# Stacking key halves for the query-key products and moving row statistics to ScalarE in a gated cross-attention and expert kernel

## The chip, the cores and the metric

One core of a Trainium2 chip runs the whole program in one launch. The metric is the device time of that launch in microseconds (us), lower is better. TensorE does the matrix products, VectorE, ScalarE and GpSimd the elementwise work, SyncE only issues DMAs. The profile names them PE, DVE, ACT, POOL and SP.

## The reference

Input: 32 batches of 256 rows with 256 features, and for each batch 77 context rows with 192 features. The layer is a gated cross-attention with 8 heads of 64, then a gated mixture of experts:

```python
q = (layernorm(x) @ Wq).reshape(b, n, 8, 64)
k = (context @ Wk).reshape(b, m, 8, 64)
v = (context @ Wv).reshape(b, m, 8, 64)
attn = softmax(einsum('bihd,bjhd->bhij', q, k) * 64 ** -0.5)
x = x + tanh(g_xattn) * (einsum('bhij,bjhd->bihd', attn, v).reshape(...) @ Wout + bout)
y = layernorm(x)
x = x + tanh(g_ffn) * (top-2 of 16 gated experts of y + shared gated expert of y)
```

All arrays are float32. The last line, the expert part, is not touched by the change.

## The kernel before

**Products in halves.** A float32 product is made from rounded halves. Each operand is split into a rounded part `hi` (an ACT copy into a rounded 32-bit format, helper `high`, L226) and the remainder `lo` (a DVE subtraction, helper `low`, L231). The helper `products` (L71) then issues three matmuls into one PSUM bank: hi x hi (L75), one half's lo (L76) and the other half's lo (L77).

**The algebra.** The scores of one head are x Wq_h K_h^T. The kernel never makes the queries: it makes K = context Wk for a pair of heads (128 rows, 64 for each head), and from it M_h = Wq_h K_h^T for each head, for four batches at once (4 x 77 = 308 columns). The scores are then x times M. The layer norm of x enters as follows: the mean is taken out of Wq once, and the reciprocal standard deviation of each row, `rstd1`, is the scale of the exponential.

**How Wq is laid out.** `wq_hi` and `wq_lo` hold 128 partitions for each head; 64 of them are that head's rows and the other 64 are zeros, because `kT` holds two heads on its 128 partitions. A *query-key unit* (`query_keys`, L281) is the product of half of one head's Wq (128 columns) with `kT`: three matmuls of 128x308.

**Stages.** `prepare` (L332) loads and splits the weights, makes K and M for the first group of four batches and the statistics of the first 16 tiles of 128 rows. `attend` (L550) runs 8 groups g of 4 batches; b is the batch and q its place in the group. `mix` and `passes` are the expert part.

**One batch of `attend`.** The order on each engine is written out by hand, and semaphores tie the engines together. TensorE, for batch b: scores of the first 128 rows; two query-key units for the next group; attention times values of batch b-1 (`attend_values`, 24 matmuls in two banks); scores of the second 128 rows; two more query-key units; transposes of the first half's probabilities (8, L723); the output projection of b-1 (24 matmuls); K for a pair of heads (5 matmuls); V of this batch (5 matmuls); transposes of the second half's probabilities. Units are made in groups 0 to 6 and K in 27 of the 32 batches (groups 0 to 5, and three batches of group 6).

ScalarE, in this order: `xT_hi`, `ctxb_hi`, two `M_hi`, the exponential of the first half (L782), two `OT_hi`, two `M_hi`, the exponential of the second half, two `PT_hi` of the first half, `kT_hi`, `V_hi`, two `PT_hi` of the second half.

VectorE, in this order: `row_max` (L834) and the subtraction of it (L837) for the first half, two `M_lo`, one `bn_stats`, `row_sum` (L844) and its reciprocal (L847), two `OT_lo`; then the same with `row_max`, the subtraction, two `M_lo`, one `bn_stats` and `row_sum` for the second half, two `PT_lo` of the first half, the residual of b-1 (two additions and two `bn_stats`), `kT_lo`, `V_lo`, two `PT_lo` of the second half. PT is the transposed probabilities, OT the attention output, transposed.

GpSimd makes xT_lo and other remainders, multiplies the probabilities by 1 / row_sum (L646), adds the bias, and at the end of a group turns the statistics into `rstd1` with 20 small chained instructions (`rstd_on_gpsimd`, L138).

**Statistics ahead.** In groups 0 to 5 SyncE loads, for batch b, the 256 rows of batch b+8 into `x_ahead` (two buffers). `stats_ahead` (L873) makes their mean and variance with two `bn_stats` on VectorE, one for each 128 rows.

**Waits that matter here.** `attend_values` of b waits for the last `PT_lo` of b and for `V_lo`. A query-key unit waits for `kT_lo` (K_lo) and for its bank to be read (M_lo). Transposes wait for GpSimd's normalisation and for the `PT_lo` that reads the same bank. `row_max` waits for the scores.

Of the kernel before, what the change touches and what calls it, by code (L numbers as in the profile page):

```python
# [28 lines left out]
P = 128  # L29
# [9 lines left out]
GB = 4  # L39
# [95 lines left out]
LN_STEPS = 6 + 2 + 3 * 4  # L135


def rstd_on_gpsimd(nc, pool, stats, rstd, var, work, chain, before):  # L138
# [8 lines left out]
    g = nc.gpsimd  # L147
    link(g.tensor_tensor(work, stats[:, :, 1], stats[:, :, 4], ALU.subtract))
    link(g.tensor_tensor(work, work, work, ALU.mult))
    link(g.tensor_scalar(work, work, 0.25, LN_EPS, ALU.mult, ALU.add))  # L150
    link(g.tensor_tensor(var, stats[:, :, 2], stats[:, :, 5], ALU.add))
    link(g.tensor_scalar(var, var, 1.0 / D, None, ALU.mult))
    link(g.tensor_tensor(var, var, work, ALU.add))
# [8 lines left out]

def attention_tensors(nc, c, ctx):
# [5 lines left out]
    a.kT = [sb(f"kT_{s}", [P, GK], F32R) for s in ("hi", "lo")]  # L169
# [6 lines left out]
    a.stats1 = sb("stats1", [P, TILES * 6])  # L176
# [117 lines left out]
def make_M(nc, pe, c, a, n, pair, k):  # L294
    pe.wait_ge(a.K_lo, n + 1)
    wait(pe, a.M_lo, 4 * n + k - 1)
    query_keys(nc, c, a, a.ps_proj[k % 2][:, 0:GK], a.kT, pair, k)


def high_K(nc, act, a, n):  # L300
    act.wait_ge(a.K_done, n + 1)
    wait(act, a.M_done, 4 * n)
    high(nc, a.kT[0][:, :], a.ps_proj[1][:, 0:GK], a.K_hi)


# [26 lines left out]
def prepare(nc, c, a):  # L332
# [5 lines left out]
    with ExitStack() as ctx:  # L338
# [3 lines left out]
        kT = [a.kT, [sb(f"kT2_{s}", [P, GK], F32R) for s in ("hi", "lo")]]  # L342
# [20 lines left out]
        def head_rows(w, j):  # L363

            return w[j * DH:(j + 1) * DH, :].rearrange("p (q j) d -> p q j d", j=2)[:, :, j, :]

        with nc.Block() as block:  # L367
# [34 lines left out]
            def _(pool):  # L402
# [3 lines left out]
                for w in (c.wq_hi, c.wq_lo):  # L406
                    nc.gpsimd.memset(f32(w[:, :, :]), 0.0).then_inc(zeroed, 1)
# [25 lines left out]
            def _(pe):  # L433
# [14 lines left out]
                key_unit(1)  # L448
                pe.wait_ge(wq_lo_done, 2)
# [10 lines left out]
            def _(act):  # L460
# [37 lines left out]
            def _(v):  # L498
# [51 lines left out]
def attend(nc, c, a):  # L550


    with ExitStack() as ctx:
# [7 lines left out]
        var1, work1 = sb("var1", [P, 4 * GB]), sb("work1", [P, 4 * GB])  # L561
        ps_proj = a.ps_proj
# [17 lines left out]
        ahead_stats, rstd_chain, rstd_ready = sem("ahead_stats"), sem("rstd_chain"), sem("rstd_ready")  # L580
# [17 lines left out]
        with nc.Block() as block:  # L598
# [42 lines left out]
            def _(pool):  # L641
# [7 lines left out]
                def rstd_of(first, tiles, before):  # L649
                    stats = a.stats1[:, bass.ds(first * 6, tiles * 6)].rearrange("p (t s) -> p t s", s=6)  # L650
# [1053 lines left out]
```

## Time and profile before

| what | value |
|---|---|
| time, median of 3 runs (lowest to highest) | 1077.92 us (1070.39 to 1084.31) |
| time of the profiled execution | 1068.79 us |
| its span, first to last instruction | 1066.6 us |
| mean granted clock of TensorE | 0.95 of full speed |
| busy: TensorE, VectorE, ScalarE, GpSimd | 86%, 75%, 44%, 47% |

The span of the profiled execution is 2.2 us shorter than its own time; what is outside is start and end of the launch. `prepare` runs from 0 to about 34 us, `attend` to about 503 us, the expert part to the end. In timeline rows the first number is the start in us from the span's start, the second the length in us; a merged row (x2, x4) gives the whole length of its instructions. What stands in square brackets is the idle time of that engine before the row and what ended it. The end of a matmul is modelled, so the pace of TensorE is read from the starts of successive rows, not from their lengths.

### The profile page before, as it was taken

Reading aid. Unit: us, or ns where it says so; the run is one execution under the profiler, and the core shown is the slowest. Engines: PE = TensorE matmul, PEld = TensorE weight load, DVE = VectorE, ACT = ScalarE, POOL = GpSimd, SP = SyncE. Lnnn points to the kernel's source line nnn. Section 1 sums busy time; section 2 is a strip of 40 time slices with the busy share of each in tenths; the row PEclk is TensorE's granted clock in tenths of the full one; section 3 lists DMA queues with packets and bytes.
Section 4 is the critical chain, followed back from the end, with each engine's and each line's share of the span. In section 5 each row is a group of like instructions: output and inputs, shape, how many; then the busy total and the mean of one; then the engine's idle time right before and its main releaser. Section 6 shows DMA issues by size and latency. Waiting matters only on the chain. (4 is left out here: it accounts for less than half of the span.)

```text
span 1066.6 us, 20998 instructions
## 1 busy us (share of the span) xinstructions
PE 916.2 (86%) x6728; PEld 857.1 (80%) x6729; DVE 797.5 (75%) x1824; ACT 471.9 (44%) x967; POOL 506.0 (47%) x635
## 2 busy tenths in 40 slices
PE   4799999999999999997599999973868784788883
PEld 3699999999999999986588888862857773778783
DVE  5699999999899999886588888882636563466563
ACT  4456555555555555542644554430323231333331
POOL 7546453545545454441235555551435545155555
PEclk9799999999999999999599999996989998799997
DMA  7213232222323211211524444455887872767660
GB/s 221 68 44 97 86 98 86 72 74 81 98 86 97 74 54 57 66 53 60 173 94 172 162 168 166 149 209 199 317 298 254 279 252 82 238 213 220 216 202 23
DMA packets 108326, 150.94 MB, mean 142 GB/s; under 512 B 21830, under 2 KB 72394, under 8 KB 108240
## 3 DMA queue, kind: packets, MB, share of 16 engines
q1 hardware_dynamic: 92880, 107.60, 33.0%
q0 software_dynamic: 15360, 42.24, 10.4%
q8 instruction: 49, 0.80, 0.3%
q14 instruction: 37, 0.30, 0.1%
HBM read 90.19 MB, written 65.90 MB: 146 GB/s over the span
## 5 line engine op out<-in xcount | busy, mean ns | idle before, releaser
L646 POOL TENSOR_TENSOR prob<-prob,row_sum 128x616 f32<-128x616 f32 x64 | 77.9, 1217 | 132.9 <-DVE row_sum L847 132.6
L1482 POOL DMA_INDIRECT rows_scratch<-prow x80 | 78.7, 984 | 98.0 <-DVE prow L1618 78.9
L75 PE MATMUL ps_h<-w_flat,eyT_hi 128*128 x320 | 98.8, 309 | 27.6 <-DVE eyT_lo L1600 24.3
L1482 POOL DMA_INDIRECT out<-prow x80 | 78.7, 983 | 76.9 <-DVE prow L1618 53.5
L1575 ACT ACTIVATE eyT_hi<-ps_ey 128x512 fp32r<-128x512 f32 x80 | 48.2, 602 | 145.9 <-PE ps_ey L1504 90.9
L1074 POOL DMA_INDIRECT rows_scratch<-row,slot x64 | 67.9, 1061 | 75.5 <-DVE row L1321 60.9
L1504 PE MATMUL ps_ey<-ident,prow 128*128 128x128 f32 x320 | 52.2, 289 | 51.2 <-DMA prow<-rows_scratch 44.2
L1600 DVE TENSOR_TENSOR eyT_lo<-ps_ey,eyT_hi 128x512 fp32r<-128x512 f32 x80 | 54.9, 686 | 54.3 <-ACT eyT_hi L1575 52.2
L1618 DVE TENSOR_TENSOR prow<-ps_z,prow 128x512 f32<-128x512 f32 x80 | 54.7, 685 | 53.4 <-PE ps_z L77 26.5
L76 PE MATMUL ps_h<-w_flat,eyT_hi 128*128 x320 | 91.1, 285 | 0.0
L77 PE MATMUL ps_h<-w_flat,eyT_lo 128*128 x320 | 90.8, 284 | 0.0
L75 PEld LDWEIGHTS ps_h<-w_flat,eyT_hi 128*128 128x128 f32 x320 | 62.6, 196 | 33.4 <-issue 33.0
L75 PE MATMUL ps_s<-M_hi,xT_hi 128*128 128x308 f32 x256 | 81.1, 317 | 5.0 <-PEq L367 4.1
L262 POOL TENSOR_TENSOR xT_lo<-xT_raw,xT_hi 128x512 fp32r<-128x512 f32 x32 | 41.3, 1289 | 92.5 <-ACT ctxb_hi L228 91.4
L1504 PEld LDWEIGHTS ps_ey<-ident,prow 128*128 128x128 f32 x320 | 38.3, 148 | 55.3 <-DMA prow<-rows_scratch 45.6
L1607 DVE SCALAR_TENSOR_TENSOR a<-ps_h,prow,silu 128x128 f32<-128x128 f32 x160 | 48.4, 344 | 43.9 <-issue 18.5
L233 DVE TENSOR_TENSOR PT_lo<-ps_pt,PT_hi 77x512 fp32r<-77x512 f32 x128 | 80.3, 667 | 0.0
L76 PE MATMUL ps_s<-M_lo,xT_hi 128*128 128x308 f32 x256 | 78.4, 306 | 0.0
L77 PE MATMUL ps_s<-M_hi,xT_lo 128*128 128x308 f32 x256 | 78.3, 306 | 0.0
L75 PE MATMUL ps_o<-wo_hi,OT_hi 128*128 128x256 f32 x256 | 74.6, 291 | 1.4 <-DVE OT_lo L233 1.4
L75 PE MATMUL ps_o<-PT_hi,V_hi 96*128 96x256 f32 x256 | 72.9, 285 | 3.3 <-DVE PT_lo L233 3.3
L228 ACT ACTIVATE M_hi<-ps_proj 128x308 fp32r<-128x308 f32 x112 | 47.7, 429 | 56.7 <-PE ps_proj L77 56.1
(263 smaller groups left out, 3418.0 us busy)
## 6 DMA issues: line engine op xcount, KB each, us to landing
prow<-rows_scratch SPq DMA_DIRECT2D x160, 258.0 KB
rows_scratch<-blank SPq DMA_DIRECT2D x34, 258.0 KB, 2.9
xT_raw<-in_xT SPq DMA_DIRECT2D x32, 256.0 KB, 4.4
x_tok<-in_x SPq DMA_DIRECT2D x32, 256.0 KB, 2.9
x_scratch<-x_tok SPq DMA_DIRECT2D x32, 256.0 KB, 3.2
row<-x_scratch SPq DMA_DIRECT2D x16, 512.0 KB, 3.9
x_ahead<-in_x SPq DMA_DIRECT2D x26, 256.0 KB, 4.4
w_raw<-in_W SPq DMA_DIRECT2D x16, 256.0 KB
```

The source lines that it names most:

```text
L75: nc.tensor.matmul(out, lh, rh, start=start and n == 0, stop=False)
L76: nc.tensor.matmul(out, lh, rl, start=False, stop=False)
L77: last = nc.tensor.matmul(out, ll, rh, start=False, stop=stop and n == len(pairs) - 1)
L233: nc.vector.tensor_tensor(lo, source, f32(hi), ALU.subtract).then_inc(done, 1)
L646: nc.gpsimd.tensor_tensor(pr, pr, row_sum[i][:, :].unsqueeze(2).broadcast_to((P, H, CK)), ALU.mult).then_inc(normed, 1)
L1074: pool.indirect_dma_start(c.rows1, bass.IndirectOffsetOnAxis(slot1[:, t:t + 1], 0), row[G % NX][:, i, :], None).then_inc(scattered[G % NX] ...
L1482: pool.indirect_dma_start(dram, bass.IndirectOffsetOnAxis(target, 0), row[u][:, i, 0:columns], None, bounds_check=bound, oob_is_err=False) ...
L1504: last = nc.tensor.transpose(ps_y[u % 2][:, k, i * P:(i + 1) * P], row[u][:, i, YROW + k * P:YROW + (k + 1) * P], c.ident[:, :])
L1575: nc.scalar.activation(yT[p][0][:, :, :], ps_y[p][:, :, :], ACT.Copy).then_inc(yT_hi, 1)
L1600: V.tensor_tensor(yT[p][1][:, :, :], ps_y[p][:, :, :], f32(yT[p][0][:, :, :]), ALU.subtract).then_inc(yT_lo, 1)
L1607: V.scalar_tensor_tensor(a[p][:, i, :], ps_h[p][:, i, 0:HID], row[b][:, i, weight:weight + 1], silu[p][:, i, :], ALU.mult, ALU.mult).then_ ...
L1618: V.tensor_tensor(row[b][:, :, 0:D], ps_z[p][:, :, :], row[b][:, :, 0:D], ALU.add).then_inc(final, 1)
```

## The change

Two parts.

**Keys and remainder in one operand.** `kT` is now one tile for each of the two heads of a pair. For head 0 its partitions 0 to 63 hold the rounded keys and partitions 64 to 127 hold the remainder of the same keys; for head 1 it is the other way round. `wq_hi` holds a head's rows in both halves of the partitions, `wq_lo` in the one half that meets the rounded keys, with zeros in the other. A query-key unit is two matmuls: Wq_hi times the stacked operand gives hi x hi + hi x lo, Wq_lo times it gives lo x hi. To write it, each K needs two ACT copies and two DVE subtractions of 64x308 where one of each of 128x308 stood. In `prepare`, ScalarE writes `wq_hi` with four copies of 64x1024 (two before), and GpSimd clears only `wq_lo`.

**Statistics on ScalarE.** The two `bn_stats` of a batch of groups 0 to 5 leave VectorE. ScalarE issues four activations of 128x256 with an accumulator output in their place: Identity with scale -1/256 for two tiles (minus the mean), and Square with the minus mean as bias for two tiles (the sum of squares). Their elementwise outputs go to unused bfloat16 tiles. They stand between the exponential of the second half and the `PT_hi` of the first half. GpSimd's chain for these groups has 15 instructions in place of 20. The statistics in `prepare` stay on VectorE.

```diff
 def query_keys(nc, c, a, out, kT, pair, k):
-    h, cc = 2 * pair + k // 2, k % 2
-    products(nc, out, [
-        (c.wq_hi[:, h, cc * P:(cc + 1) * P], c.wq_lo[:, h, cc * P:(cc + 1) * P],
-         kT[0][:, :], kT[1][:, :])]).then_inc(a.M_done, 1)
+    h, cc, both = 2 * pair + k // 2, k % 2, kT[k // 2][:, :]
+    nc.tensor.matmul(out, c.wq_hi[:, h, cc * P:(cc + 1) * P], both, start=True, stop=False)
+    nc.tensor.matmul(out, c.wq_lo[:, h, cc * P:(cc + 1) * P], both, start=False, stop=True).then_inc(a.M_done, 1)
+
+def half(j):
+    return slice(j * DH, (j + 1) * DH)
+
+def high_keys(nc, a, kT, bank):
+    for j in range(2):
+        high(nc, kT[j][half(j), :], bank[half(j), :], a.K_hi)
+
+def low_keys(nc, v, a, n, kT, bank):
+    for j in range(2):
+        v.wait_ge(a.K_hi, 2 * n + j + 1)
+        low(nc, kT[j][half(1 - j), :], kT[j][half(j), :], bank[half(j), :], a.K_lo)
...
 def make_M(nc, pe, c, a, n, pair, k):
-    pe.wait_ge(a.K_lo, n + 1)
+    pe.wait_ge(a.K_lo, 2 * n + 2)
...
+                def stats_ahead(b, b_half, par):
+                    act.wait_ge(a.ahead_in[par], 16 * (b_half + 1))
+                    for i in range(2):
+                        t = 2 * (b + 2 * GB) + i
+                        nc.scalar.activation(unused[i][:, :], a.x_ahead[par][:, i, :], ACT.Identity, scale=-1.0 / D,
+                                             accum_out=less_mean[:, t:t + 1]).then_inc(ahead_mean, 1)
+                    wait(act, ahead_stats, 2 * b)
+                    for i in range(2):
+                        t = 2 * (b + 2 * GB) + i
+                        act.wait_ge(ahead_mean, 2 * b + i + 1)
+                        nc.scalar.activation(unused[2 + i][:, :], a.x_ahead[par][:, i, :], ACT.Square,
+                                             bias=less_mean[:, t:t + 1],
+                                             accum_out=squares[:, t:t + 1]).then_inc(ahead_stats, 1)
...
                         exponentials(b, 1)
+                        if exists(g + 2):
+                            stats_ahead(b, 2 * g + q // 2, q % 2)
                         high_PT(b, 0)
...
                             low_M_units(b, g, q, 0)
-                        if exists(g + 2):
-                            stats_ahead(b, 2 * g + q // 2, q % 2, 0)
                         sums(b, 0)
...
                             low_M_units(b, g, q, 1)
-                        if exists(g + 2):
-                            stats_ahead(b, 2 * g + q // 2, q % 2, 1)
                         sums(b, 1)
```

The next rows are ScalarE's instructions of `attend` from the exponential of a batch's second half on, in the kernel before; L228 is the helper `high`.

```order
L782 ACTIVATE prob<-prob,rstd 128x616
L228 ACTIVATE PT_hi<-ps_pt 77x4x128 x2
L228 ACTIVATE kT_hi<-ps_proj 128x308
L228 ACTIVATE V_hi<-ps_proj 77x4x2x64
L228 ACTIVATE PT_hi<-ps_pt 77x4x128 x2
```

The same place in the changed kernel, where L246 is `high` and L816 the exponential:

```order
L816 ACTIVATE prob<-prob,rstd 128x616
L829 ACTIVATE unused,less_mean<-x_ahead 128x256
L829 ACTIVATE unused,less_mean<-x_ahead 128x256
L835 ACTIVATE unused,squares<-x_ahead,less_mean 128x256
L835 ACTIVATE unused,squares<-x_ahead,less_mean 128x256
L246 ACTIVATE PT_hi<-ps_pt 77x4x128 x2
L246 ACTIVATE kT<-ps_proj 64x308
L246 ACTIVATE kT<-ps_proj 64x308
L246 ACTIVATE V_hi<-ps_proj 77x4x2x64
L246 ACTIVATE PT_hi<-ps_pt 77x4x128 x2
```

Four activations now stand ahead of `PT_hi`, and the copy of the keys is two.

VectorE's instructions from the subtraction of the second half's maximum to the next batch's `row_max`, in the kernel before:

```order
L837 TENSOR_TENSOR prob<-ps_s,row_max 128x616
L233 TENSOR_TENSOR M_lo<-ps_proj,M_hi 128x4x77 x2
L876 BN_STATS stats<-x_ahead 128x6
L844 TENSOR_REDUCE row_sum<-prob 128x8
L847 RECIPROCAL row_sum<-row_sum 128x8
L233 TENSOR_TENSOR PT_lo<-ps_pt,PT_hi 77x4x128 x2
L858 TENSOR_TENSOR x_tok<-ps_o,x_tok 128x256
L861 BN_STATS stats<-x_tok 128x6
L858 TENSOR_TENSOR x_tok<-ps_o,x_tok 128x256
L861 BN_STATS stats<-x_tok 128x6
L233 TENSOR_TENSOR kT_lo<-ps_proj,kT_hi 128x308
L233 TENSOR_TENSOR V_lo<-ps_proj,V_hi 77x4x2x64
```

And in the changed kernel, where L251 is `low`:

```order
L888 TENSOR_TENSOR prob<-ps_s,row_max 128x616
L251 TENSOR_TENSOR M_lo<-ps_proj,M_hi 128x4x77 x2
L895 TENSOR_REDUCE row_sum<-prob 128x8
L898 RECIPROCAL row_sum<-row_sum 128x8
L251 TENSOR_TENSOR PT_lo<-ps_pt,PT_hi 77x4x128 x2
L909 TENSOR_TENSOR x_tok<-ps_o,x_tok 128x256
L912 BN_STATS stats<-x_tok 128x6
L909 TENSOR_TENSOR x_tok<-ps_o,x_tok 128x256
L912 BN_STATS stats<-x_tok 128x6
L251 TENSOR_TENSOR kT<-ps_proj,kT 64x308 x2
L251 TENSOR_TENSOR V_lo<-ps_proj,V_hi 77x4x2x64
```

The `bn_stats` behind `M_lo` is gone (so is the one in the first half of the batch), and the subtraction of the keys is two.

## Rows read from the trace of the kernel before

**Rows 1.** The page: TensorE's granted clock in 40 slices of the span.

```profile
PEclk9799999999999999999599999996989998799997
```

**Rows 2.** Busy time by stretch: groups 0 to 5, 6, and 7.

```profile
core 0: us, PE busy (x) PEld busy (x) DVE busy (x) ACT busy (x) POOL busy (x), PEclk, DMA share, GB/s
...
64.00:180.00 116.00, 116.00 (x885) 112.42 (x884) 107.48 (x210) 66.15 (x131) 56.87 (x93) 1.00 0.29 84
...
411.00:440.00 29.00, 29.00 (x221) 27.98 (x221) 25.95 (x50) 16.20 (x32) 11.37 (x13) 1.00 0.21 61
...
453.90:493.00 39.10, 37.91 (x283) 34.69 (x282) 32.26 (x58) 17.62 (x33) 14.86 (x15) 1.00 0.16 50
```

**Rows 3.** Timeline of DVE in group 2, from one second half to the next.

```profile
203.48 0.80 DVE L834 TENSOR_REDUCE row_max<-ps_s 128x8 f32<-128x616 f32 x1 [0.36 <-PE ps_s L77]
...
205.03 0.85 DVE L233 TENSOR_TENSOR M_lo<-ps_proj,M_hi 128x308 fp32r<-128x308 f32 x2
205.80 0.42 DVE L876 BATCH_NORM_STATS2 stats<-x_ahead 128x6 f32<-128x256 f32 x1
...
207.06 1.24 DVE L233 TENSOR_TENSOR PT_lo<-ps_pt,PT_hi 77x512 fp32r<-77x512 f32 x2
...
217.94 0.80 DVE L834 TENSOR_REDUCE row_max<-ps_s 128x8 f32<-128x616 f32 x1 [0.38 <-PE ps_s L77]
```

**Rows 4.** Timeline of PE in group 2, one query-key unit.

```profile
203.28 0.31 PE L75 MATMUL ps_proj<-kT_hi,wq_hi 128*128 128x308 f32 x1
203.42 0.31 PE L76 MATMUL ps_proj<-kT_lo,wq_hi 128*128 128x308 f32 x1
```

**Rows 5.** Timeline of DVE in group 7, with neither units, keys nor statistics ahead.

```profile
461.31 0.80 DVE L834 TENSOR_REDUCE row_max<-ps_s 128x8 f32<-128x616 f32 x1 [0.30 <-PE ps_s L77]
...
464.77 1.23 DVE L233 TENSOR_TENSOR PT_lo<-ps_pt,PT_hi 77x512 fp32r<-77x512 f32 x2
...
469.29 0.79 DVE L834 TENSOR_REDUCE row_max<-ps_s 128x8 f32<-128x616 f32 x1
...
474.30 0.80 DVE L834 TENSOR_REDUCE row_max<-ps_s 128x8 f32<-128x616 f32 x1 [0.33 <-PE ps_s L77]
```

**Rows 6.** Timeline of PE in group 7, the first matmul of `attend_values`.

```profile
469.42 0.39 PE L75 MATMUL ps_o<-PT_hi,V_hi 96*128 96x256 f32 x1 [0.41 <-DVE PT_lo L233]
```

**Rows 7.** Timeline of ACT in group 2.

```profile
205.14 0.81 ACT L782 ACTIVATE prob<-prob,rstd 128x616 f32<-128x616 f32 x1 [0.39 <-DVE prob L837]
205.86 1.06 ACT L228 ACTIVATE PT_hi<-ps_pt 77x512 fp32r<-77x512 f32 x2
...
211.36 0.63 ACT L228 ACTIVATE xT_hi<-xT_raw 128x512 fp32r<-128x512 f32 x1
211.89 0.33 ACT L228 ACTIVATE ctxb_hi<-ctxb_raw 128x154 fp32r<-128x154 f32 x1
```

**Rows 8.** Groups by form, 60 to 480 us: busy us, mean ns of one, idle before.

```profile
L228 ACT ACTIVATE PT_hi<-ps_pt 77x512 fp32r<-77x512 f32 x119 | 63.3, 582 | 0.0
...
L228 ACT ACTIVATE ctxM_hi<-ctx_raw 128x616 fp32r<-128x616 f32 x6 | 4.3, 714 | 0.0
```

**Rows 9.** Timeline of `prepare`: the shortest activation, with two columns.

```profile
13.22 0.20 ACT L469 ACTIVATE tanh_g<-gates 128x2 f32<-128x2 f32 x1 [2.99 <-DMA bias<-in_bout]
```

**Rows 10.** Timeline of DVE: second halves of batches 0, 1, 26 and 27.

```profile
43.97 0.75 DVE L834 TENSOR_REDUCE row_max<-ps_s 128x8 f32<-128x616 f32 x1
...
59.13 0.80 DVE L834 TENSOR_REDUCE row_max<-ps_s 128x8 f32<-128x616 f32 x1 [0.36 <-PE ps_s L77]
...
420.75 0.80 DVE L834 TENSOR_REDUCE row_max<-ps_s 128x8 f32<-128x616 f32 x1 [0.37 <-PE ps_s L77]
...
435.19 0.80 DVE L834 TENSOR_REDUCE row_max<-ps_s 128x8 f32<-128x616 f32 x1 [0.38 <-PE ps_s L77]
```

**Rows 11.** Timeline of DVE at the end of `prepare`.

```profile
32.92 0.41 DVE L516 BATCH_NORM_STATS2 stats<-x_ahead 128x6 f32<-128x256 f32 x1
```

**Rows 12.** Timeline of PE: the first scores of `attend`.

```profile
34.63 0.59 PE L75 MATMUL ps_s<-M_hi,xT_hi 128*128 128x308 f32 x1 [4.11 <-PEq L367]
```

More of the change, by code:

```diff
@@ L135, with linked @@
 LN_STEPS = 6 + 2 + 3 * 4
-def rstd_on_gpsimd(nc, pool, stats, rstd, var, work, chain, before):
+LN_AHEAD_STEPS = 1 + 2 + 3 * 4
+def linked(pool, chain, before):
     step = [0]
@@ L145, in link, with newton @@
         pool.wait_ge(chain, before + step[0])
[L147 to L153, printed above, removed]
+    return link
+def newton(g, link, rstd, var, work):
     link(g.tensor_scalar(rstd.bitcast(I32), var.bitcast(I32), -0.5, float(SEED), ALU.mult, ALU.add))
@@ L160, in rstd_on_gpsimd, with rstd_of_stats, rstd_of_squares @@
         link(g.tensor_tensor(rstd, rstd, work, ALU.mult))
+def rstd_of_stats(nc, pool, stats, rstd, var, work, chain, before):
+    g, link = nc.gpsimd, linked(pool, chain, before)
+    link(g.tensor_tensor(work, stats[:, :, 1], stats[:, :, 4], ALU.subtract))
+    link(g.tensor_tensor(work, work, work, ALU.mult))
+    link(g.tensor_scalar(work, work, 0.25, LN_EPS, ALU.mult, ALU.add))
+    link(g.tensor_tensor(var, stats[:, :, 2], stats[:, :, 5], ALU.add))
+    link(g.tensor_scalar(var, var, 1.0 / D, None, ALU.mult))
+    link(g.tensor_tensor(var, var, work, ALU.add))
+    newton(g, link, rstd, var, work)
+def rstd_of_squares(nc, pool, squares, rstd, var, work, chain, before):
+    g, link = nc.gpsimd, linked(pool, chain, before)
+    link(g.tensor_scalar(var, squares, 1.0 / D, LN_EPS, ALU.mult, ALU.add))
+    newton(g, link, rstd, var, work)
 def attention_tensors(nc, c, ctx):
@@ L402, in _ @@
             def _(pool):
-                for w in (c.wq_hi, c.wq_lo):
-                    nc.gpsimd.memset(f32(w[:, :, :]), 0.0).then_inc(zeroed, 1)
+                nc.gpsimd.memset(f32(c.wq_lo[:, :, :]), 0.0).then_inc(zeroed, 1)
                 pool.wait_ge(wk_hi_done, 1)
@@ L463, in _ @@
                 high_group(nc, act, a, 0)
-                act.wait_ge(zeroed, 2)
                 act.wait_ge(centred, 4)
-                for j in range(2):
-                    high(nc, head_rows(c.wq_hi, j), wq_raw[j * DH:(j + 1) * DH, :, :], wq_hi_done)
+                for at in (0, 1):
+                    for j in range(2):
+                        high(nc, head_rows(c.wq_hi, j, j ^ at), wq_raw[half(j), :, :], wq_hi_done)
                 act.wait_ge(gates_in, 48)
@@ L561, in attend @@
         var1, work1 = sb("var1", [P, 4 * GB]), sb("work1", [P, 4 * GB])
+        less_mean, squares = sb("less_mean", [P, TILES]), sb("squares", [P, TILES])
+        unused = [sb(f"unused{i}", [P, D], BF16) for i in range(4)]
         ps_proj = a.ps_proj
```

48 lines of the change are left out of this document (22 added, 26 removed).

## The prediction

> **What bounds the kernel now.** I read the busy time by stretch first, since the change touches only `prepare` and `attend`. In groups 0 to 5 TensorE is busy for 116.00 of 116.00 us, VectorE for 107.48, ScalarE for 66.15 [rows 2]. So TensorE bounds `attend`, with VectorE close behind. The timeline of VectorE then gives the period of a batch: the second half's `row_max` starts at 203.48 and again at 217.94, 14.46 us apart, and both times VectorE had waited 0.36 to 0.38 us for TensorE's scores [rows 3]. A full engine says nothing of the chain behind it, so the next thing to find is the loop through the other engines and how far it is below 14.46.
>
> Group 7 shows that loop bare. It has no units, no keys and no statistics, and there TensorE waits 0.41 us for `PT_lo` in each batch [rows 6]. One turn, from `row_max` at 461.31: (1) subtraction, exponential, `row_sum`, reciprocal, until `PT_lo` starts at 464.77: 3.46. (2) VectorE alone, with `PT_lo`, residual, `V_lo`, `PT_lo` in one run until the next `row_max` at 469.29: 4.52. (3) to the first matmul of `attend_values` at 469.42: 0.13 [rows 6]. (4) TensorE makes `attend_values` and scores, and the next second-half `row_max` starts at 474.30: 4.88. Together 12.99, exactly 474.30 less 461.31 [rows 5].
>
> In group 2 the same loop has one `kT_lo` more in part (2). A pair of `M_lo` of the same shape moves VectorE on by 0.77 (205.03 to 205.80), so one costs 0.39. Part (1) is 207.06 less 203.48 = 3.58 [rows 3]. That gives 3.58 + 4.91 + 0.13 + 4.88 = 13.50. So 0.96 us of slack lie under TensorE's 14.46.
>
> **TensorE's side.** One matmul of a unit starts 0.14 us behind the other (203.28, 203.42) [rows 4]; its length of 0.31 overlaps with the next. Each batch loses four of them, 0.57 us, so TensorE's own period falls to 13.89. Over the 28 batches with units that is at most 16 us, 1.5% of the time.
>
> **VectorE's side.** Two `bn_stats` leave; one moves the engine on by about 0.33, but `row_sum` behind it must still wait for the exponential (0.81 from 205.14 to 205.95 [rows 7]), so the second one gives only about 0.1 in part (1). The second subtraction of keys adds 0.39: it has half the partitions, but as many columns, 308, and I take the time by columns. The first `bn_stats` and its DMA wait are off this loop.
>
> **ScalarE's side, which decides.** The four activations stand between the exponential and `PT_hi`, and the engine works in order. Before, the exponential starts 1.66 us after `row_max` (203.48, 205.14), `PT_hi` follows 0.72 later at 205.86 [rows 3, 7], and the first one takes 0.58 [rows 8] plus 0.04 to wake VectorE, which is assumed: no row here prices the step alone, and the 0.13 of part (3) is above it. With S for the four activations `PT_lo` can start 1.66 + 0.72 + S + 0.58 + 0.04 = 3.00 + S after `row_max`. `row_sum` has long been done by then, so this takes the place of part (1). The changed loop is
>
> 3.00 + S + (4.52 + 0.77) + 0.13 + 4.88 = 13.30 + S.
>
> It equals the old period at S = 1.16 and TensorE's new one at 0.59.
>
> What is S? An activation of 154 columns takes 0.33 and one of 512 takes 0.63, so 256 take 0.42; the next starts 0.10 before the end (211.89 against 211.99) [rows 7], which leaves 0.32. The Square takes its bias from a tile. The exponential takes its scale from one and needs 0.81 for 616 columns [rows 7], where a copy of 616 needs 0.714 [rows 8]: 0.10 more, 0.41. So the four are 0.64 + 0.82 = 1.46 without the accumulator. No row of this trace shows what writing an accumulator costs. The nearest is the shortest activation, two columns in 0.20 [rows 9]: overlapped as the others it moves the engine on by 0.10, with nothing overlapped on either side 0.30. It can also be free. I take 0.10, since the other activations overlap: S = 1.86, with ends at 1.28 (no pointer cost either, four times 0.32) and 2.66. The waits on `ahead_mean` cost nothing I can see: the mean of tile 0 is made while that of tile 1 runs. The load of `x_ahead` has the whole batch to land.
>
> So the period becomes 15.16, +0.70. VectorE then waits about 1.2 us for `PT_hi` in each batch, and TensorE stands still for 15.16 - 13.89 = 1.27 us ahead of `attend_values` and the unit that waits for `V_lo`.
>
> **The sum.** Statistics run in batches 0 to 23. The step from batch 0 to 1 takes 15.16 already (43.97 to 59.13) [rows 10] and has no residual, so it hides them: 23 steps of +0.70 = +16.1. In group 6 there are none, and the period of 14.44 (420.75 to 435.19) [rows 10] is TensorE's; the loop there is 12.99 + 0.77 = 13.76, below 13.87. Three steps win 0.57: -1.7. Group 7 has no units: 0. In `prepare` five K cost VectorE 0.39 more each, up to 1.9; VectorE ends at 33.33 [rows 11], `attend` begins at 34.63 [rows 12], and the matmuls saved there are behind it, so I take +1.1 with ends 0 and 1.9. The extra `wq_hi` copies are ahead of keys that come later, the shorter GpSimd chain is off the loop: 0. The sum is +15.5 us.
>
> The profiled execution took 1068.79, so its like would be 1084.3. It is 9.1 below the median of the runs, 1077.92; the same +15.5 on the median gives 1093.4, which I predict. That is 1.4% up. A measurement of this kernel tells about 2% from no change, 21.6 us.
>
> Bounds: S = 1.28 gives +0.12 a batch, +2.8 - 1.7 + 0 = +1, 1079. S = 2.66 gives +1.50 a batch, +34.5 - 1.7 + 1.9 = +34.7, 1112.6. Runs scatter by some us, so I give 1076 to 1111.
>
> **Rivals.**
>
> *The accumulator costs more (chance 0.25).* If each output costs 0.17 or more, S passes 2.12 and the kernel is slower by over 2%. At 0.25 each, S = 2.46: +1.30 a batch, 29.9 - 1.7 + 1.1 = +29, 1107. For it: the write depends on the very activation before it, so overlap is not sure. Against: in these rows neighbours overlap also where one is tiny work.
>
> *The statistics are short, and the kernel is not slower (0.18).* Place: the same four activations; price: S; it decides at S = 1.16. Output to bfloat16, or an accumulating pass that writes faster, could halve the 0.83 ns a column: 0.21 and 0.31 each, 1.04 with a free accumulator. Then the loop is 14.34: 23 times -0.12 = -2.8, -1.7, +1.1 = -3.4, 1074.5. For it: no row has a bfloat16 output. Against: the columns per ns are the same here for copies and the exponential, within 0.10 in 616. Even S = 0 would win only 23 x 0.57 + 1.7 - 1.1 = 14 us, 1.3%, so faster by over 2% needs something I don't see.
>
> *The clock (0.05).* The granted clock stays at 1.00, the level of 2.4 GHz, through group 7, though TensorE is idle there for 1.2 of 39.1 us in waits of 0.4 [rows 2]; it is below the top in slices around the start of `attend` [rows 1], where TensorE stands still for 4.11 us at once [rows 12]. The changed kernel has 1.27 us of them in each batch. At 1.2 GHz part (4) would be longer by up to 4.7, so a tenth of the stretch at that level costs 0.5 a batch, +11: 1104. The Trainium skill (TensorE: Matmul & The Clock Gate, "A second HAM failure mode: psum-queue depth-cycling") speaks against the change here: frequent short idles between groups of matmuls can make the clock swing between its levels. By that rule the time would be the 1104; the trace, at 1.00 with idles of 0.4 us, does not bear it out so far.
>
> **How the numbers follow.** Forecast 0.52, rivals 0.25, 0.18 and 0.05. Slower by over 2%: the first rival and half of the third, 0.28. Faster by over 2%: 0.02. Within 2%: 0.70.
>
> **What would show it.** Right: timeline rows of VectorE with an idle of 1.0 to 1.5 us before `PT_lo` of the first half, ended by ScalarE's `PT_hi`; four activations moving ScalarE on by 1.86 in all; TensorE waiting for `PT_lo` ahead of `attend_values`; `row_max` 15.1 to 15.2 us apart in groups 0 to 5, 13.9 in group 6, 13.0 in group 7; TensorE's share below 93% there. Wrong: no idle before `PT_lo`, or a period at or below 14.4 in groups 1 to 5 (then S or the loop is wrong); 64x308 subtractions that take half the time; a clock below 1.00 inside `attend`; a change of time in the expert part, of which I expect none.

## The result and the profile after

| | time before | time after | ratio, 95% interval |
|---|---|---|---|
| median | 1077.93 us (4 runs, 1070.39 to 1084.31) | 1101.96 us (4 runs, 1097.02 to 1105.34) | 1.0224 (1.0190 to 1.0258) |

The kernel became slower by 24.0 us. That it is slower is clear of the scatter; whether by more than 2% is not, since the interval holds 1.02. The forecast was 15.5 us; 1101.96 lies inside the range given. The profiled execution took 1097.02 us, its span is 1095.3 us.

The busy time of groups 0 to 5 and of 42 us of group 6, in the changed kernel, answers to [rows 2]:

```profile
core 0: us, PE busy (x) PEld busy (x) DVE busy (x) ACT busy (x) POOL busy (x), PEclk, DMA share, GB/s
64.00:180.00 116.00, 107.48 (x791) 100.31 (x789) 101.33 (x191) 75.57 (x188) 50.84 (x79) 1.00 0.29 84
411.00:453.00 42.00, 42.00 (x317) 40.09 (x317) 39.50 (x76) 24.90 (x51) 16.47 (x17) 1.00 0.21 62
```

TensorE, full before, is busy for 107.48 of 116.00 us (92.7%). It is idle for 8.5 us there, and its granted clock is still 1.00. No engine is full in this stretch any more. So the bound is no engine but a chain through several, and the share of busy time can't name it. The timeline of VectorE in group 2 does; it answers to [rows 3]:

```profile
213.33 0.80 DVE L885 TENSOR_REDUCE row_max<-ps_s 128x8 f32<-128x616 f32 x1 [0.31 <-PE ps_s L77]
...
214.88 0.85 DVE L251 TENSOR_TENSOR M_lo<-ps_proj,M_hi 128x308 fp32r<-128x308 f32 x2
215.84 0.80 DVE L895 TENSOR_REDUCE row_sum<-prob 128x8 f32<-128x616 f32 x1
216.67 0.20 DVE L898 RECIPROCAL row_sum<-row_sum 128x8 f32<-128x8 f32 x1
218.11 1.29 DVE L251 TENSOR_TENSOR PT_lo<-ps_pt,PT_hi 77x512 fp32r<-77x512 f32 x2 [1.23 <-ACT PT_hi L246]
...
220.54 0.43 DVE L912 BATCH_NORM_STATS2 stats<-x_tok 128x6 f32<-128x256 f32 x1
221.00 0.98 DVE L251 TENSOR_TENSOR kT<-ps_proj,kT 64x308 fp32r<-64x308 f32 x2
222.01 0.69 DVE L251 TENSOR_TENSOR V_lo<-ps_proj,V_hi 77x512 fp32r<-77x512 f32 x1
...
223.81 0.78 DVE L885 TENSOR_REDUCE row_max<-ps_s 128x8 f32<-128x616 f32 x1
...
228.82 0.80 DVE L885 TENSOR_REDUCE row_max<-ps_s 128x8 f32<-128x616 f32 x1 [0.32 <-PE ps_s L77]
```

Read it as the loop of the prediction. Part (1), 213.33 to 218.11, is 4.78. It ends with an idle of 1.23 us for ScalarE's `PT_hi`, which [rows 3] do not have. Part (2), to `row_max` at 223.81, is 5.70; the rest, to 228.82, is 5.01. The period is 15.49, where it was 14.46.

The same place on ScalarE, which answers to [rows 7]:

```profile
215.00 0.81 ACT L816 ACTIVATE prob<-prob,rstd 128x616 f32<-128x616 f32 x1 [0.64 <-DVE prob L888]
215.72 0.40 ACT L829 ACTIVATE unused<-x_ahead 128x256 bf16<-128x256 f32 x1
216.02 0.19 ACT L829 ACTIVATION_READ_ACCUMULATOR unused<-x_ahead 128x1 f32 x1
216.12 0.40 ACT L829 ACTIVATE unused<-x_ahead 128x256 bf16<-128x256 f32 x1
...
216.51 0.49 ACT L835 ACTIVATE unused<-x_ahead,less_mean 128x256 bf16<-128x256 f32 x1
216.91 0.19 ACT L835 ACTIVATION_READ_ACCUMULATOR unused<-x_ahead,less_mean 128x1 f32 x1
217.01 0.49 ACT L835 ACTIVATE unused<-x_ahead,less_mean 128x256 bf16<-128x256 f32 x1
...
217.50 1.06 ACT L246 ACTIVATE PT_hi<-ps_pt 77x512 fp32r<-77x512 f32 x2
```

`PT_hi` starts at 217.50, where the first of the four activations starts at 215.72: they cost 1.78 us, forecast 1.86. Each accumulator output is an instruction of its own in the trace, 0.19 long, and moves the engine on by 0.09 to 0.10.

The waits of all `attend` (60 to 500 us), by what ended them:

```profile
engine line waited for: us in total, times, longest us
...
DVE PT_lo L251 <- ACT PT_hi L246: 28.3, 23, 1.2
...
PE ps_proj L302 <- DVE V_lo L251: 16.2, 23, 0.7
...
PE ps_o L75 <- DVE PT_lo L251: 9.2, 25, 0.4
DVE row_max L885 <- PE ps_s L77: 9.0, 29, 0.3
```

Reading it from top to bottom gives the loop: ScalarE is late for VectorE, VectorE for TensorE, TensorE for VectorE's next `row_max`. The first row has 23 waits, one for each batch with statistics from 1 to 23.

**Where the 24 us came from.** The second half's `row_max` of a batch dates it in both traces. In the changed kernel it starts at 44.66 (batch 0), 58.54 (1), 414.65 (24), 457.00 (27) and 508.87 (31); in the kernel before at 43.97, 59.13, 391.91, 435.19 and 487.28 (rows of the same timeline; [rows 10] have three of them).

| stretch | forecast | measured |
|---|---|---|
| `prepare` and batch 0, to its second `row_max` | +1.1 | +0.7 |
| step 0 to 1 | 0 | -1.3 (13.88 for 15.16) |
| steps 1 to 24, 23 of them | +16.1 | +23.3 |
| steps 24 to 27 | -1.7 | -0.9 (42.35 for 43.28) |
| steps 27 to 31 | 0 | -0.2 |
| expert part, from batch 31 | 0 | +7.1, in this one execution |

The last row is within the scatter: experiments 1 to 4 below, with the same expert part, took 595, 581, 584 and 579 us for it; before took 579 and after 586. By the difference of the medians, 24.0, about 2 us are left for it. What the sum missed lies in the third row, and it is 0.31 us in each batch.

### The profile page after: what moved, and what is told of

The parts are those of the page before. It is cut to its first block and busy times, and to the rows that moved or that the text cites. A ratio compares the mean times of both kernels' runs of the same rounds, so it can differ in the third digit from the quotient of the medians.

```text
span 1095.3 us, 20944 instructions
## 1 busy us (share of the span) xinstructions
PE 917.8 (84%) x6600; PEld 847.1 (77%) x6601; DVE 802.6 (73%) x1808; ACT 522.7 (48%) x1193; POOL 497.1 (45%) x604
## 5 line engine op out<-in xcount | busy, mean ns | idle before, releaser
L75 PE MATMUL ps_h<-w_flat,eyT_hi 128*128 x320 | 101.0, 316 | 31.2 <-DVE eyT_lo L1641 25.3
L251 DVE TENSOR_TENSOR PT_lo<-ps_pt,PT_hi 77x512 fp32r<-77x512 f32 x128 | 81.5, 676 | 29.6 <-ACT PT_hi L246 29.6
L76 PE MATMUL ps_h<-w_flat,eyT_hi 128*128 x320 | 93.6, 293 | 0.0
L77 PE MATMUL ps_h<-w_flat,eyT_lo 128*128 x320 | 93.1, 291 | 0.0
L816 ACT ACTIVATE prob<-prob,rstd 128x616 f32<-128x616 f32 x64 | 51.9, 811 | 74.6 <-DVE prob L888 74.6
L75 PE MATMUL ps_o<-PT_hi,V_hi 96*128 96x256 f32 x256 | 76.3, 298 | 11.8 <-DVE PT_lo L251 11.7
L246 ACT ACTIVATE M_hi<-ps_proj 128x308 fp32r<-128x308 f32 x112 | 41.9, 426 | 71.2 <-PE ps_proj L303 71.2
```

The lines of the kernel that those rows point to most:

```text
L75: nc.tensor.matmul(out, lh, rh, start=start and n == 0, stop=False)
L76: nc.tensor.matmul(out, lh, rl, start=False, stop=False)
L77: last = nc.tensor.matmul(out, ll, rh, start=False, stop=stop and n == len(pairs) - 1)
L251: nc.vector.tensor_tensor(lo, source, f32(hi), ALU.subtract).then_inc(done, 1)
L816: nc.scalar.activation(prob[i][:, :], prob[i][:, :], ACT.Exp, scale=c.rstd1[:, bass.ds(2 * b + i, 1)]).then_inc(exp_done, 1)
```

## The experiments

All ratios are against the kernel before, on the same chip. The first four kernels ran on a chip where the kernel before takes 1075.39 us, close to the runs above; experiments 5 and 7 ran on a second (1016.80 us) and 6 and 8 on a third (1019.86 us). The periods in `attend` agree between the chips (in group 7, which no edit touches, a batch takes 12.94 to 13.01 us in every experiment after its first step), so experiments are compared by their periods and by ratios, never by times across chips. What no edit touches reads the same on both: the idle before `PT_lo` is 1.23 in experiment 5 as in the change, and parts (3) and (4) are 4.98 for 5.01. Three theories stood at the start. The place: the four activations cost the time because they are ahead of `PT_hi` in ScalarE's order. The work: ScalarE or a slower product would cost it anywhere. For what was missed in part (2): a price of the key subtractions.

**1. The four activations elsewhere** (`e1_stats_behind_OT`). The same instructions, ahead of the second half's `M_hi`, where ScalarE waited for TensorE (69.0 us of such waits in `attend`).

```diff
                             high_OT(b - 1)
+                        if exists(g + 2):
+                            stats_ahead(b, 2 * g + q // 2, q % 2)
                         if not last:
                             high_M_units(b, g, q, 1)
                         exponentials(b, 1)
-                        if exists(g + 2):
-                            stats_ahead(b, 2 * g + q // 2, q % 2)
                         high_PT(b, 0)
```

> The four statistics activations move from ahead of the first half's PT_hi to behind OT_hi, where ScalarE waits about 1.4 us for TensorE's units in the changed kernel. Theory (the loop through PT_hi: its place on ScalarE is what costs): PT_lo of the first half starts 3.46 us after row_max again, the loop is 3.46 + 5.70 + 5.01 = 14.1 to 14.2 us in groups 0 to 5, the same as in group 6, against 15.49; the time falls by 1.33 x 23 = 31 us under the changed kernel, to about 0.7 to 0.9% under the kernel before. Rival (the amount of work given to ScalarE costs, wherever it stands, or the waits of TensorE for V_lo come from elsewhere): the period stays at 15 us or above and the kernel stays slower than before.

Measured: 1067.17 us, ratio 0.9923 (0.9886 to 0.9961). VectorE in group 2:

```profile
199.90 0.80 DVE L885 TENSOR_REDUCE row_max<-ps_s 128x8 f32<-128x616 f32 x1 [0.29 <-PE ps_s L77]
...
203.37 1.24 DVE L251 TENSOR_TENSOR PT_lo<-ps_pt,PT_hi 77x512 fp32r<-77x512 f32 x2
...
209.03 0.79 DVE L885 TENSOR_REDUCE row_max<-ps_s 128x8 f32<-128x616 f32 x1
...
214.03 0.80 DVE L885 TENSOR_REDUCE row_max<-ps_s 128x8 f32<-128x616 f32 x1 [0.32 <-PE ps_s L77]
```

`PT_lo` has no idle before it and starts 3.47 after `row_max`; part (2) is 5.66; the period is 14.13. The activations themselves still take 1.79 in ScalarE's trace. So their place cost 1.36 a batch, and not the work: the rival falls, and with two lines moved a kernel that was 2.2% slower is 0.8% faster. Part (2) is 0.04 shorter than the 5.70 above, and that too belongs to the wait: VectorE moves on by 1.20 over the two `PT_lo` where it had waited for `PT_hi`, by 1.16 where it had not.

**2. Keys alone** (`e2_keys_alone`). The two-matmul units and stacked keys, with the statistics as `bn_stats` on VectorE as before.

```diff
                         exponentials(b, 1)
-                        if exists(g + 2):
-                            stats_ahead(b, 2 * g + q // 2, q % 2)
                         high_PT(b, 0)
...
                             low_M_units(b, g, q, 0)
+                        if exists(g + 2):
+                            bn_ahead(b, 2 * g + q // 2, q % 2, 0)
                         sums(b, 0)
```

> Only the stacked keys with two products; the statistics ahead stay on VectorE as bn_stats. Theory: no activations ahead of PT_hi, so part (1) of the loop is 3.58 as before, the loop 3.58 + 5.70 + 5.01 = 14.3 us; TensorE alone would allow 13.9. So 14.3 against 14.47 before, about 4 us faster in groups 0 to 5 and 1 in group 6: 0.3 to 0.6% under the kernel before. Rival (the keys' two subtractions are what made the change slow): a period above 14.47 and a time above that of before.

Measured: 1067.2 us, ratio 0.9940 (0.9911 to 0.9969). The period is 14.28 (201.00 to 215.28): 3.59, 5.66 and 5.03. The stacked operand alone is a gain, a small one: 0.6%, with an interval that stays below 1.

**3. Statistics alone** (`e3_stats_alone`). Products and keys as before, statistics on ScalarE ahead of `PT_hi`.

```diff
-    h, cc, both = 2 * pair + k // 2, k % 2, kT[k // 2][:, :]
-    nc.tensor.matmul(out, c.wq_hi[:, h, cc * P:(cc + 1) * P], both, start=True, stop=False)
-    nc.tensor.matmul(out, c.wq_lo[:, h, cc * P:(cc + 1) * P], both, start=False, stop=True).then_inc(a.M_done, 1)
+    h, cc = 2 * pair + k // 2, k % 2
+    products(nc, out, [
+        (c.wq_hi[:, h, cc * P:(cc + 1) * P], c.wq_lo[:, h, cc * P:(cc + 1) * P],
+         kT[0][:, :], kT[1][:, :])]).then_inc(a.M_done, 1)
```

> Only the statistics on ScalarE, ahead of PT_hi; three products and one subtraction of the keys as before. Theory: 4.78 + 4.91 + 5.01 = 14.70 us for the loop, just over TensorE's 14.46, so about 0.24 x 23 = 5 to 6 us slower than before, 0.5%. The two parts of the change then don't add up: 0.24 for the one and -0.2 for the other alone, +1.0 together, since each alone is largely within the slack. Rival (the statistics cost about the whole +1.0 by themselves): a period of 15.3 us or more and over 1.5% slower than before.

Measured: 1081.57 us, ratio 1.0077 (1.0042 to 1.0111). VectorE in group 2:

```profile
205.24 0.80 DVE L871 TENSOR_REDUCE row_max<-ps_s 128x8 f32<-128x616 f32 x1 [0.30 <-PE ps_s L77]
...
210.02 1.29 DVE L251 TENSOR_TENSOR PT_lo<-ps_pt,PT_hi 77x512 fp32r<-77x512 f32 x2 [1.23 <-ACT PT_hi L246]
...
212.46 0.43 DVE L898 BATCH_NORM_STATS2 stats<-x_tok 128x6 f32<-128x256 f32 x1
212.80 0.46 DVE L251 TENSOR_TENSOR kT_lo<-ps_proj,kT_hi 128x308 fp32r<-128x308 f32 x1
213.18 0.68 DVE L251 TENSOR_TENSOR V_lo<-ps_proj,V_hi 77x512 fp32r<-77x512 f32 x1
...
214.97 0.79 DVE L871 TENSOR_REDUCE row_max<-ps_s 128x8 f32<-128x616 f32 x1
...
219.98 0.80 DVE L871 TENSOR_REDUCE row_max<-ps_s 128x8 f32<-128x616 f32 x1 [0.32 <-PE ps_s L77]
```

The same wait of 1.23 stands there, and the period is 14.74. The two parts of the change do not add up: against 14.46 the keys alone are -0.18, the statistics alone +0.28, both +1.03. In the loop they nearly do. It was 13.50 by the prediction's reading, 0.96 below TensorE's 14.46. The keys alone bring it to 14.28, which is +0.78; the statistics alone to 14.74, +1.24; both to 15.49, +1.99, where the two add up to 2.02. The slack of 0.96 is there only once, so 2.02 less 0.96 is what shows. The pair of rows at 212.80 and 213.18 against those at 221.00 and 222.01 above shows where the missing 0.31 of each batch is: one `kT_lo` of 128x308 moves VectorE on by 0.38, the two of 64x308 by 1.01, and they also start 0.46 behind the `bn_stats` before them where this one starts 0.34 behind.

**4. Four activations more** (`e4_four_more`). Identity with an accumulator four times more at the same place, into tiles of their own; nothing reads them.

```diff
+                    wait(act, again_done, 4 * b)
+                    for i in range(4):
+                        nc.scalar.activation(more[i][:, :], a.x_ahead[par][:, i % 2, :], ACT.Identity, scale=-1.0 / D,
+                                             accum_out=again[:, 4 * b + i:4 * b + i + 1]).then_inc(again_done, 1)
                     wait(act, ahead_stats, 2 * b)
```

> The changed kernel with four more Identity activations with accumulator outputs into unused tiles at the same place, extra work whose results nothing uses; each moves ScalarE on by 0.40, 1.60 in all. Theory: the place is on the loop with no slack left, so every microsecond shows: period 15.49 + 1.60 = 17.1 us. Rival (another wait bounds the period and the statistics are only near it): the period grows by less than 1.2 us.

Measured, one run: 1128.93 us, ratio 1.050, period 17.07 (`PT_lo` at 204.41 and at 221.48), and VectorE's idle grows from 1.23 to 2.83:

```profile
204.41 1.28 DVE L251 TENSOR_TENSOR PT_lo<-ps_pt,PT_hi 77x512 fp32r<-77x512 f32 x2 [2.83 <-ACT PT_hi L246]
...
221.48 0.69 DVE L251 TENSOR_TENSOR PT_lo<-ps_pt,PT_hi 77x512 fp32r<-77x512 f32 x1 [2.83 <-ACT PT_hi L246]
```

Four times 0.40 on ScalarE are +1.60, and the period gained 1.58. ScalarE's time ahead of `PT_hi` goes into the period whole.

**5. The key subtractions in one half of the partitions each** (`e5_same_partitions`). In the change a subtraction reads one half of the partitions and writes the other. Here each reads and writes the same half, so the remainder that it writes is the other head's: the kernel computes other keys, of the same shapes.

```diff
-        v.wait_ge(a.K_hi, 2 * n + j + 1)
-        low(nc, kT[j][half(1 - j), :], kT[j][half(j), :], bank[half(j), :], a.K_lo)
+        v.wait_ge(a.K_hi, 2 * n + 2)
+        low(nc, kT[j][half(1 - j), :], kT[1 - j][half(1 - j), :], bank[half(1 - j), :], a.K_lo)
```

> The changed kernel, with each 64x308 subtraction reading and writing the same 64 partitions (it makes the other head's remainder, so this part of the result is another one). Open point: in the changed kernel the pair and what follows take 1.18 us more than nothing, where one 128x308 took 0.39 and two were forecast at 0.77. Theory A (the shift between partition halves costs): the pair moves VectorE on by 0.77 again, part (2) is 5.3, the period 15.1 us. Theory B (an instruction on 64 partitions doesn't overlap with its neighbours, as the two 64x308 copies on ScalarE, 0.43 apart where 128x308 are 0.32 to 0.34 apart and which shift nothing): the pair stays at 1.0 to 1.1, the period at 15.5 us.

Measured, one run: 1037.65 us, ratio 1.021, period 15.37 (213.56 to 228.93):

```profile
205.42 0.43 DVE L912 BATCH_NORM_STATS2 stats<-x_tok 128x6 f32<-128x256 f32 x1
205.88 0.98 DVE L251 TENSOR_TENSOR kT<-ps_proj,kT 64x308 fp32r<-64x308 f32 x2
206.79 0.67 DVE L251 TENSOR_TENSOR V_lo<-ps_proj,V_hi 77x512 fp32r<-77x512 f32 x1
```

The keys start at 205.88 and `V_lo` at 206.79, 0.91 for the pair where it was 1.01; part (2) is 5.59 for 5.70. Neither theory has its number: of the 0.41 by which part (2) was missed, the crossing explains 0.11 at most. The three places where one instruction follows another (into the pair, within it, out of it) suggested a third: an instruction starts about 0.12 us later, behind the end of the one before it, where the first partition of its operands differs from that one's. It differs at three places in the change, at two here, at none in the kernel before. In the change it is only the output of the first subtraction that starts elsewhere, and only inputs that differ between the second and `V_lo`.

**6. Both subtractions on partitions 0 to 63** (`e7_both_low_half`), to test that. Both make the first head's remainder, one of them into a spare tile, so the second head's keys have none in `attend`. The work is the same, and so are the shapes.

```diff
-    low_keys(nc, v, a, n, a.kT, a.ps_proj[1][:, 0:GK])
+    v.wait_ge(a.K_hi, 2 * n + 2)
+    for out in (a.kT[1], a.K_spare):
+        low(nc, out[half(0), :], a.kT[0][half(0), :], a.ps_proj[1][half(0), 0:GK], a.K_lo)
```

> The changed kernel, but in attend both 64x308 subtractions read and write partitions 0 to 63 (the remainder of the first head only, once into the second head's tile and once into a spare one, so the remainders are not those of the change). With the same partitions as input and output the handoff to V_lo had overlapped, the two before it had not. Theory C (the overlap of about 0.10 us with the instruction before is lost where the first partition of an operand changes, not for 64 partitions as such): all three handoffs overlap, the pair moves VectorE on by 0.77 to 0.80 from the start of the first to V_lo, part (2) is 5.3, the period 15.1 us. Theory B (64 partitions as such): the second still starts 0.50 us behind the first, the period stays at 15.3 to 15.5 us.

Measured, one run: 1033.15 us, ratio 1.013, period 15.11 (210.06 to 225.17):

```profile
202.18 0.43 DVE L915 BATCH_NORM_STATS2 stats<-x_tok 128x6 f32<-128x256 f32 x1
202.52 0.45 DVE L252 TENSOR_TENSOR kT<-ps_proj,kT 64x308 fp32r<-64x308 f32 x1
202.90 0.46 DVE L252 TENSOR_TENSOR K_spare<-ps_proj,kT 64x308 fp32r<-64x308 f32 x1
203.29 0.67 DVE L252 TENSOR_TENSOR V_lo<-ps_proj,V_hi 77x512 fp32r<-77x512 f32 x1
```

The pair takes 0.77, as much as the forecast had, the `bn_stats` is followed after 0.34 again, and part (2) is 5.34. That is 0.36 below the 5.70 of the change: three places, 0.12 each; experiment 5 with two of them is 0.25 above it. So half the partitions cost what all do, and the missing time is the overlap that neighbours lose. Both experiments are single runs, but their loops repeat: the 22 steps from batch 1 to 23 are 15.34 to 15.40 us in experiment 5, 15.09 to 15.14 here and 15.45 to 15.52 in the change. This edit also takes away the wait for the second copy of the keys between the two subtractions. That is not what brings the overlap back: the first subtraction and `V_lo` still stand behind a wait of their own here, and they overlap with what is ahead of them (they start 0.34 and 0.39 behind it, and it is 0.43 and 0.46 long). The period of 15.11 stands beside a forecast of 15.16.

**7. The remainders on GpSimd** (`e6_keys_on_gpsimd`), the first try at a version that beats both. Experiment 1, and the key subtractions leave VectorE: ScalarE copies K out of its bank, and GpSimd subtracts.

```diff
+    nc.scalar.activation(a.K_raw[:, :], a.ps_proj[1][:, 0:GK], ACT.Copy).then_inc(a.K_copied, 1)
     high_keys(nc, a, a.kT, a.ps_proj[1][:, 0:GK])
...
                         norm(b, 1)
+                        if makes_K(g, q):
+                            pool.wait_ge(normed, 2 * b + 2)
+                            low_K(nc, pool, a, b + GB + 1)
```

> The statistics behind OT_hi as in the experiment before, and in attend the keys' remainder made by GpSimd from a copy of the keys that ScalarE writes to SBUF (one more activation of 128x308 ahead of the two copies). Theory: part (2) of the loop falls from 5.70 to 4.52, the loop to about 13.0, so TensorE's own work bounds the period at 13.9 us, 0.57 under before, in groups 0 to 6: about 14 us, 1.2 to 1.4% under the kernel before. Rival (GpSimd becomes late: two subtractions of 0.85 us behind the second half's normalisation, with the chain for the reciprocal standard deviation behind them once a group): TensorE waits for the keys or for normalised probabilities, and the period is above 14.1 us.

Measured: 1009.38 us, ratio 0.9924 (0.9898 to 0.9949), no better than experiment 1. Within a group the step is 13.81 to 13.87 (200.78 to 214.65 is 13.87), but the step into the next group is 15.31 (214.65 to 229.96). TensorE there:

```profile
214.88 0.31 PE L304 MATMUL ps_proj<-kT,wq_lo 128*128 128x308 f32 x1
216.37 1.10 PE L767 MATMUL ps_pt<-ident,prob 128*77 128x128 f32 x8 [1.18 <-POOL prob L688]
```

And GpSimd, whose key remainders now end where the chain for `rstd1` begins:

```profile
206.67 1.75 POOL L346 TENSOR_TENSOR kT<-K_raw,kT 64x308 fp32r<-64x308 f32 x2 [1.04 <-ACT kT L247]
208.51 0.20 POOL L177 TENSOR_SCALAR var<-squares 128x8 f32<-128x8 f32 x1
...
212.60 0.20 POOL L159 TENSOR_TENSOR rstd<-rstd,work 128x8 f32<-128x8 f32 x1
212.98 1.30 POOL L281 TENSOR_TENSOR xT_lo<-xT_raw,xT_hi 128x512 fp32r<-128x512 f32 x1 [0.18 <-POOL rstd L159]
...
215.10 1.21 POOL L688 TENSOR_TENSOR prob<-prob,row_sum 128x616 f32<-128x616 f32 x1
```

The chain runs from 208.51 to 212.80, `xT_lo` and two small ones follow, and the normalisation of the probabilities, for which TensorE's transposes wait, starts only at 215.10. Against experiment 1, with 14.13 a step, the three other steps of a group win 0.9 us together and this one loses 1.2.

**8. The chain in three pieces** (`e8_chain_in_pieces`). Experiment 7, with the 15 small instructions spread over three batches of the next group, 5 in each; `rstd1` is needed a group later only.

```diff
-                        rstd_of_squares(nc, pool, squares[:, tiles], c.rstd1[:, tiles], var1[:, 0:2 * GB],
-                                        work1[:, 0:2 * GB], rstd_chain, LN_STEPS + LN_AHEAD_STEPS * g)
-                        pool.sem_inc(rstd_ready, 1)
...
+                            for step in steps[5 * q:5 * q + 5]:
+                                link(step())
+                            if q == 2:
+                                pool.sem_inc(rstd_ready, 1)
```

> Statistics behind OT_hi, the keys' remainder on GpSimd, and GpSimd's chain of 15 for the reciprocal standard deviation in three pieces of 5 behind the keys of three batches of the next group, where the run before had it whole at the end of a group and TensorE then waited 1.2 us for the first normalised probabilities of the next. Theory: the long step of 15.3 us at each start of a group goes, all steps of groups 1 to 6 are 13.9 us, TensorE's own work; about 8 us less than the run before, 1.5 to 1.7% under the kernel before. Rival (GpSimd has no room for a piece either): TensorE waits for normalised probabilities in the batches with a piece, and nothing or less than 3 us is won.

Measured: 1003.27 us against 1019.86, ratio 0.9831 (0.9799 to 0.9863). The steps from batch 1 to 27 are 13.81 to 13.88, those into a new group too:

```profile
211.73 0.80 DVE L913 TENSOR_REDUCE row_max<-ps_s 128x8 f32<-128x616 f32 x1 [0.39 <-PE ps_s L77]
...
225.60 0.80 DVE L913 TENSOR_REDUCE row_max<-ps_s 128x8 f32<-128x616 f32 x1 [0.38 <-PE ps_s L77]
```

and TensorE is full again (columns as in the windows above):

```profile
64.00:180.00 116.00, 116.00 (x887) 112.13 (x886) 104.54 (x194) 87.43 (x220) 69.73 (x97) 1.00 0.31 90
```

These 26 steps take 359.87 us, 16.2 less than the 376.06 of the kernel before; the medians differ by 16.6. This is the whole gain that two matmuls for three can bring here, the "at most 16 us" of the prediction. The kernel is 1.4 to 2.0% faster than the one before, and so faster than the changed one.

## Why the prediction was right, and where its sum was off

**Direction and mechanism: right.** The loop was read bare in group 7 and laid over the other groups, and ScalarE's four activations were put into its part (1). After: an idle of 1.23 us before `PT_lo` (forecast about 1.2), ended by `PT_hi`; S = 1.78 (1.86); part (1) 4.78 = 3.00 + S to the hundredth; parts (3) and (4) together 5.01, as 0.13 + 4.88; TensorE's share 92.7% (below 93%); group 7 at 12.96 to 12.99 (13.0). The 0.04 that was assumed for waking VectorE fits too: `PT_lo` starts 0.61 after the first `PT_hi`, which takes 0.58. Two signs missed: `row_max` is 15.49 apart in groups 1 to 5, not 15.1 to 15.2, and 14.1 in group 6, not 13.9. Experiment 1 shows that the place is the cause, experiment 4 that ScalarE's time there goes into the period one for one, and experiment 6, without the term that was mis-sized, stands at 15.11 where 15.16 was forecast.

**The accumulator.** No row of before had it; 0.10 was taken between 0 and 0.30. It is 0.09 to 0.10. The rival with more than 0.17 falls, and so does the one in which the statistics are short: 256 columns took 0.40, and 0.49 with a pointer, though the output was bfloat16. The Trainium skill (ScalarE: Activation LUTs, "What ACT_TABLE_LOAD costs") gives 186 ns plus 0.833 ns a column, and about 93 ns more for each pointer operand; for 256 columns an estimate from it is 0.40 and 0.49, and this trace agrees with both.

**The step that failed** is "The second subtraction of keys adds 0.39: it has half the partitions, but as many columns, 308, and I take the time by columns". The time by columns was right (0.38 and 0.39 in experiment 6), but the duration came from a pair of `M_lo` that start at the same partition as their neighbours. Where the first partition changes, the overlap with the instruction before is lost: part (2) took 5.70, not 5.29. Of the 0.41, 0.36 are gone in experiment 6; the other 0.05 are mostly the 0.04 that the two `PT_lo` take more behind a wait (experiment 3, with one `kT_lo`, has 4.95 for 4.91). The 0.41, less the 0.08 by which S was too high, is the 0.33 between 15.49 and 15.16: over 23 steps 7.6 us, where 7.2 were missed (23.3 less 16.1). The sum passed the bound of 2% (21.6 us) by this term, and the chance for slower by over 2%, 0.28, had been worked out from the accumulator and the clock, neither of which came. That 1101.96 lies in the range is in part luck: its bounds were made from S, whose forecast was good, and no bound was set for the subtractions. Its upper end, 1111, is also below the 1112.6 worked out for S = 2.66.

**Group 6** gained 0.9 in three steps, not 1.7, by the same term. The prediction had the loop at 13.76 there, below TensorE's 13.87. In the changed kernel:

```profile
442.89 0.80 DVE L885 TENSOR_REDUCE row_max<-ps_s 128x8 f32<-128x616 f32 x1 [0.29 <-PE ps_s L77]
...
446.35 1.23 DVE L251 TENSOR_TENSOR PT_lo<-ps_pt,PT_hi 77x512 fp32r<-77x512 f32 x2
...
452.01 0.79 DVE L885 TENSOR_REDUCE row_max<-ps_s 128x8 f32<-128x616 f32 x1
...
457.00 0.80 DVE L885 TENSOR_REDUCE row_max<-ps_s 128x8 f32<-128x616 f32 x1 [0.31 <-PE ps_s L77]
```

3.46, 5.66 and 4.99 make 14.11. The loop is above 13.87 and bounds this group too. TensorE's 42.00 of 42.00 us busy, in the windows above, don't show that. The ends of matmuls are modelled, and an idle this short can lie under them: the last matmul of a unit starts at 451.86 and the first of `attend_values` at 452.15, 0.29 later, where the last two of the unit are 0.14 apart (451.72, 451.86). TensorE's weight loads show the wait, 0.7 us for `PT_lo` in three waits of this group.

**The step from batch 0 to 1** was forecast unchanged and took 1.28 less. TensorE's clock differs there: from 44 to 49 us the granted clock is 0.54 in the kernel before and 0.77 in the changed one. The same step takes 13.83, 12.92 and 13.92 in experiments 1, 2 and 3, at 0.78, 0.85 and 1.00 in that stretch, so the shorter step is no single accident; what moves the clock there stays open. **`prepare`** cost 0.7, inside 0 to 1.9. With the same `prepare`, experiments 1, 2 and 4 reach the second `row_max` of batch 0 at 44.90, 45.53 and 45.87, and experiment 3, with that of before, at 44.07; so the +1.1 fits, and one trace can't place it closer. **The expert part** was rightly left out.

**The clock rival** (0.05) fell. The granted clock is 1.00 from 64 to 180 us, the level of 2.4 GHz, with about 1.1 us of idle in each batch (8.5 us over 116.00 / 15.49 = 7.5 batches). By the Trainium skill (TensorE: Matmul & The Clock Gate, "A second HAM failure mode: psum-queue depth-cycling") frequent short idles between groups of matmuls can make the clock swing; no stretch of groups 1 to 5 in these runs shows it, not even in experiment 4, where TensorE is busy for 99.32 of 116.00 us at 1.00.

## What to carry to other kernels

Before taking work off a full engine, find the loop through the others and how far it is below that engine's period: here two edits that add 0.78 and 1.24 to the loop had 0.96 us of slack between them. Each alone showed as -0.18 and +0.28, and both as +1.03. On an engine that works in order, cheap extra work goes where that engine waits anyway, never ahead of an instruction that others wait for; two lines moved were worth 1.36 in each of 23 batches, 31 us. When one engine is relieved, look which other's order is now tight once in every group, not only in the batch that you looked at (experiment 7 against 8).

## What the hardware showed that I had not expected

- **Overlap between VectorE's neighbours depends on the first partition.** Two subtractions of 64x308 move the engine on by 0.77 where all start at partition 0, by 0.91 with two changes of the first partition around them, by 1.01 with three, and with two or three the first is put off by 0.12 too: about 0.12 for each change (part (2) 5.34, 5.59, 5.70). Three orders of instructions were tried, so this is what these rows have in common and no more.
- **ScalarE does the same, it seems.** Its two copies of keys, 64x308 in different halves, are 0.43 apart in a merged row of 0.86, where the pair of `M_hi` of 128x308 takes 0.75 in all. The four copies to `wq_hi` in `prepare`, 64x1024 in changing halves, take 4.28 together, 1.07 each, so nothing overlaps, where the 128x1024 copy to `wv_hi` in the kernel before, 1.05 long, is followed after 0.95. That was seen, not tested by itself.
- **An accumulator output is a second instruction** (ACTIVATION_READ_ACCUMULATOR), 0.19 long, and it moves the engine on by 0.09 to 0.10.
